# Quantising three weight matrices block by block inside a feed-forward loop, instead of each at once

## What is computed

```python
x = x + jnp.tanh(g_xattn[0]) * _L0_xattn_ref(...)   # a decaying recurrence (scan) over the tokens
x = x + jnp.tanh(g_ffn[0]) * _L0_ffn_ref(_layernorm(x), w1, w2, w3)
x = x + jnp.tanh(g_xattn[1]) * _L1_xattn_ref(_layernorm(x), ctx, wq, bq, wkv, bkv, wp, bp)
x = x + jnp.tanh(g_ffn[1]) * _L1_ffn_ref(_layernorm(x), gamma, W)

def _L0_ffn_ref(x, w1, w2, w3):              # _bitlinear: activations to 8 bits in groups of 64, weights to signs
    h = jax.nn.silu(_bitlinear(x, w1)) * _bitlinear(x, w2)
    return _bitlinear(h, w3)

def _qdq(x):                                  # in _L1_xattn_ref: of x, o (per token) and wq, wp (per output row)
    s = jnp.maximum(jnp.max(jnp.abs(x), axis=-1, keepdims=True) / 127.0, 1e-08)
    return jnp.clip(jnp.round(x / s), -127.0, 127.0) * s

# in _L1_ffn_ref: W to -1, 0, 1 by its mean magnitude
w_scale = 1.0 / (jnp.mean(jnp.abs(W)) + _EPS)
w_q = jnp.clip(jnp.round(W * w_scale), -1.0, 1.0) / w_scale
```

## Time and profile before

| | |
|---|---|
| median of 3 runs | 979.26 us (978.27 to 980.02) |
| profiled execution | 976.9 us |
| its span, first to last instruction | 975.0 us |
| mean granted TensorE clock | 0.948 of full speed |
| instructions | 15020 |
| PE, DVE, ACT, POOL busy | 822.8, 750.3, 576.2, 487.7 us |

### The profile page before, as it was taken

The page is one execution under the profiler, slowest core; times in us unless marked ns, Lnnn a source line. Parts: engine busy times, 40 slices in busy tenths (PEclk is TensorE's granted clock), DMA queues, the critical chain, the costliest instruction groups (busy, mean ns, idle before and its releaser), DMA issues.

```text
span 975.0 us, 15020 instructions
## 1 busy us (share of the span) xinstructions
PE 822.8 (84%) x4373; PEld 354.8 (36%) x4373; DVE 750.3 (77%) x1492; ACT 576.2 (59%) x971; POOL 487.7 (50%) x560
## 2 busy tenths in 40 slices
PE   2898997779698978999999978799999999974654
PEld 2444543334344434445444433132323232222321
DVE  4699998788598996888888767577777777624884
ACT  3588886544445654656566554466666666665762
POOL 2857662223244433434334344476767666664761
PEclk9999999899899998999999995999999999997885
DMA  8677875523424334232322342322222221000111
GB/s 285 207 197 209 218 196 155 151 69 66 108 55 109 59 54 84 54 65 54 64 55 54 66 75 76 88 56 61 70 63 68 61 72 46 1 1 1 43 65 65
DMA packets 172381, 86.37 MB, mean 89 GB/s; under 512 B 124048, under 2 KB 156960, under 8 KB 172320
## 3 DMA queue, kind: packets, MB, share of 16 engines
q1 hardware_dynamic: 172320, 85.64, 34.8%
HBM read 37.76 MB, written 12.58 MB: 52 GB/s over the span
## 4 chain that ended last, share of the span: by engine, by line
PE 43%; DVE 15%; issue 6%; SPq 6%; DMA 5%; ACT 4%; POOL 1%; ACTq 0%; DVEq 0%; POOLq 0%
PE bank L1109 13%; PE bank L1121 6%; PE bank L1203 5%; PE bank L1174 5%; PE bank L1193 4%; DMA A<-B 3%; PE bank L1320 2%; SPq L431 2%; PE bank L1222 2%; PE bank L1212 2%; DVE bank L1529 2%; SPq L455 2%; DVE gsm L1531 1%; DVE B L1534 1%; DVE B L1540 1%
## 5 line engine op out<-in xcount | busy, mean ns | idle before, releaser
L1109 PE MATMUL bank<-A,B 128*128 128x512 f16 x1024 | 236.0, 384 | 19.7 <-DVE B L1540 11.3
L1652 DVE TENSOR_REDUCE B<-bank 128x1 f32<-128x512 f32 x256 | 168.0, 683 | 71.7 <-PE bank L1174 71.6
L947 ACT ACTIVATE A<-bank 128x512 f32<-128x512 f32 x256 | 143.8, 593 | 105.5 <-PE bank L1193 102.5
L591 POOL TENSOR_TENSOR B<-B 128x512 f16<-128x512 f32 x64 | 76.0, 1188 | 225.2 <-ACT B L814 149.3
L1109 PEld LDWEIGHTS bank<-A,B 128*128 128x128 f16 x1024 | 100.7, 99 | 146.1 <-issue 21.8
L666 POOL TENSOR_TENSOR B<-A 128x512 f32<-128x512 f32 x64 | 79.3, 1270 | 93.8 <-ACT A L947 93.8
L1121 PE MATMUL bank<-A,B 128*128 128x512 f16 x512 | 121.9, 382 | 0.0
L809 ACT ACTIVATE bank<-B 128x512 f32<-128x512 f32 x64 | 38.5, 601 | 125.2 <-DVE B L1534 125.0
L1193 PE MATMUL bank<-A 98*128 98x512 f16 x256 | 93.8, 388 | 20.6 <-ACT A L947 10.9
L1174 PE MATMUL bank<-A 96*128 96x512 f16 x256 | 98.2, 409 | 7.8 <-DMA A<-B 4.2
L666 POOL TENSOR_TENSOR B<-B,A 128x512 f32<-128x512 f32 x64 | 79.1, 1266 | 0.5 <-ACT A L947 0.5
(11 more groups left out here) (216 smaller groups left out, 1465.0 us busy)
## 6 DMA issues: line engine op xcount, KB each, us to landing
B<-in_L_ffn_w_dram SPq DMA_DIRECT2D x48, 256.0 KB, 3.7
A<-k_parts SPq DMA_DIRECT2D x48, 128.0 KB, 2.5
A<-B SPq DMA_DIRECT2D x192, 32.0 KB, 1.9
X<-in_x_dram SPq DMA_DIRECT2D x4, 1024.0 KB, 9.1
B<-in_ctx_dram SPq DMA_DIRECT2D x16, 256.0 KB, 4.4
k_parts<-B SPq DMA_DIRECT2D x16, 256.0 KB, 4.4
v_rows<-B SPq DMA_DIRECT2D x16, 256.0 KB, 2.7
B<-v_rows SPq DMA_DIRECT2D x16, 256.0 KB, 3.2
```

The lines of the kernel that those rows point to most:

```text
L591: nc.gpsimd.tensor_tensor(HLb[j][:, 1, :], Db[j % 2], HLb[j][:, 0, :], ALU.subtract).then_inc(lo_done, 1)
L947: nc.scalar.activation(PR[(HG * t + j) % 8], bank[2 + j % 2][:, :], ACT.Exp, scale=SCALE).then_inc(exp_done, 1)
L1109: last = mm(bank[2 * n + q][:, :], XQT[a][:, m, :], wt[:, m % DB, j * 512:j * 512 + 512], start=(m == 0), stop=(m == 2 * DB - 1))
L1652: reduce(NMX[g % 2][:, t, j:j + 1], bank[ROW_BANKS[r % 3]][:, :], AX.X, ALU.max, negate=True).then_inc(row_max, 1)
```

## The change

The work on the three matrices is cut into twelve blocks (m, k), m the matrix, k one of its four quarters of 512 columns, and one block is done at the end of a chunk. `matrix_work(i, j, tiles_of)` names the block of a chunk: scales of matrix 0 in tile 1 and of matrix 2 in tile 7; roundings on ScalarE in tiles 2, 5 and 8; integers on VectorE and the transposes on SyncE in the same tiles, one chunk later (so the last one in tiles 3, 6, 9). `matrix_sum` moves to the end of chunk (3,3), `mean_scale` to the end of (4,3), the mean's product on TensorE to (4,2). The next matrix is loaded behind the last transpose of the one before, at (3,0) and (6,0). The scale row is written at (9,1) and read back at (11,1). TensorE's wait for `mean_scale` moves from `q_project(0)` to `q_project(1)`, and the mean's product gets a wait for `qf_ready`. Because the blocks stand in tiles up to 9, the loops over pairs 3 to 6 are written out on TensorE, VectorE, ScalarE and GpSimd.

```diff
-        ROUNDED, SUMMED = (1, 3, 4), 2
+        ROUNDED, SUMMED = lambda m, k: DB * m + k + (1 if m == 0 else 2), DB + 1
...
+        SCALED, ROUNDED_AT, INTS, SUMMED_AT = (1, 4, 7), (2, 5, 8), (2, 5, 8), 3
+
+        def matrix_work(i, j, tiles_of):
+
+            lag = 1 if tiles_of is INTS else 0
+            return [(m, k) for m in range(3) for k in range(DB) if DB * tiles_of[m] + k + lag == FC * i + j]
...
@@ SyncE @@
-            def turn_matrix(m):
-
-                sp.wait_ge(wm_ready, m + 1)
-                for k in range(DB):
-                    sp.dma_start_transpose((WQT, WLT, WPT)[m][:, :, k * P:k * P + P], wm_ints[:, k, :]).then_inc(wm_out, 16)
-            def spread_scale():
...
+            def turn_block(m, k):
+
+                sp.wait_ge(wm_ready, DB * m + k + 1)
+                sp.dma_start_transpose((WQT, WLT, WPT)[m][:, :, k * P:k * P + P], wm_ints[:, k, :]).then_inc(wm_out, 16)
             for i in range(TOK):
-                if i in (2, 4, 6):
-                    turn_matrix(i // 2 - 1)
-                if i in (2, 4):
-                    load_matrix(i // 2)
-                if i == 6:
-                    spread_scale()
                 for j in range(FC):
                     turn_h(i, j)
+                    for m, k in matrix_work(i, j, INTS):
+                        turn_block(m, k)
+                        if k == DB - 1 and m < 2:
+                            load_matrix(m + 1)
+                    if (i, j) == (INTS[2] + 1, 1):
+                        sp.dma_start(swp_dram.rearrange("(k p) -> p k", p=P), SWQP[:, 4:8],
+                                     allow_slow_non_contiguous=True).then_inc(swp_io, 16)
+                    if (i, j) == (INTS[2] + 3, 1):
+                        sp.wait_ge(swp_io, 16)
+                        sp.dma_start(swp_all[:, :], on_all(swp_dram, D)).then_inc(swp_io, 16)
                     if j == 0 and i < TOK - 1:
                         turn_x(i + 1, (i + 1) % 2)
...
@@ ScalarE @@
+            def round_block(m, k):
+
+                if k == 0:
+                    act.wait_ge(wm_scale, m + 1)
+                scale = WS if m == 1 else RWQP[:, (0, 0, 4)[m] + k:(0, 0, 4)[m] + k + 1]
+                nc.scalar.activation(wm_raw[:, k, :], wm_raw[:, k, :], ACT.Copy, bias=RND,
+                                     scale=scale).then_inc(wm_round, 1)
...
                         high(i, j)
+                        if (i, j) == (SUMMED_AT, FC - 1):
+                            matrix_sum()
+                        for m, b in matrix_work(i, j, ROUNDED_AT):
+                            round_block(m, b)
...
@@ TensorE @@
-                if isinstance(u, int) and u == 0:
+                if u == 0:
                     pe.wait_ge(wm_out, 16 * DB)
+                if u == 1:
                     pe.wait_ge(wm_scale, 2)
...
-                        if isinstance(k, int) and k == 1 and (a, j) == (0, 2):
+                        if (i, j) == (SUMMED_AT + 1, 2):
                             pe.wait_ge(wm_round, SUMMED)
+                            pe.wait_ge(qf_ready, 1)
                             mm(bank[7][:, 0:1], ones[:, :], PART[:, 3:4], start=True, stop=True).then_inc(setup_ps, 1)
...
@@ VectorE @@
+            def scale_block(m, k):
+
+                if k == 0:
+                    dve.wait_ge(wm_in, 16 * (m + 1))
+                c = (0, 0, 4)[m]
+                last_ = reduce(ABSM[:, c + k:c + k + 1], wm_raw[:, k, :], AX.X, ALU.max, apply_absolute_value=True)
+                if k == DB - 1:
+                    link(last_)
+                    link(ts(SWQP[:, c:c + 4], ABSM[:, c:c + 4], 1.0 / 127.0, 1e-8, ALU.mult, ALU.max))
+                    recip(RWQP[:, c:c + 4], SWQP[:, c:c + 4]).then_inc(wm_scale, 1)
...
+            def ints_block(m, k):
+
+                dve.wait_ge(wm_round, ROUNDED(m, k))
+                if k == 0:
+                    up_to(dve, wm_out, 16 * DB * m)
+                raw = wm_raw[:, k, :]
+                if m != 1:
+                    ts(wm_ints[:, k, :], raw, RND, 127.0, ALU.subtract, ALU.min).then_inc(wm_ready, 1)
+                else:
+                    link(ts(raw, raw, RND, -1.0, ALU.subtract, ALU.max))
+                    ts(wm_ints[:, k, :], raw, 1.0, None, ALU.min).then_inc(wm_ready, 1)
...
+                        for m, b in matrix_work(i, j, SCALED):
+                            if m != 1:
+                                scale_block(m, b)
+                            elif b == FC - 1:
+                                mean_scale()
+                        for m, b in matrix_work(i, j, INTS):
+                            ints_block(m, b)
...
-            tiles(0, False)
-            tiles(1, False)
-            tiles(2, False)
-            with pool.Fori(3, TOK // 2 - 1) as k:
-                step.turn(12, k - 3)
-                tiles(k, False)
-            step.turns_over(TOK // 2 - 4)
-            tiles(TOK // 2 - 1, True)
+            for k in range(TOK // 2):
+                tiles(k, k == TOK // 2 - 1)
```

More of the change, by code:

```diff
@@ L447, in load_matrix @@
                 else:
-                    sp.wait_ge(wm_ready, m)
+                    sp.wait_ge(wm_ready, DB * m)
                 sp.dma_start(wm_raw, tiled((wq, wl, wp)[m])).then_inc(wm_in, 16)
-            def turn_matrix(m):
-                sp.wait_ge(wm_ready, m + 1)
-                for k in range(DB):
-                    sp.dma_start_transpose((WQT, WLT, WPT)[m][:, :, k * P:k * P + P], wm_ints[:, k, :]).then_inc(wm_out, 16)
-            def spread_scale():
[L459 to L462, removed]
+            def turn_block(m, k):
+                sp.wait_ge(wm_ready, DB * m + k + 1)
+                sp.dma_start_transpose((WQT, WLT, WPT)[m][:, :, k * P:k * P + P], wm_ints[:, k, :]).then_inc(wm_out, 16)
             load_matrix(0)
@@ L868, in tiles @@
                         c = FC * i + j
[L869 to L872, removed]
                         if j == 0 and there(i - 3):
@@ L1159, in tiles @@
                             down(i - 1, j, 1 - a)
[L1161 to L1166, removed]
+            for k in range(TOK // 2):
+                tiles(k, k == 0, k == TOK // 2 - 1)
             def rows(b, g, n):
@@ L1588, in mean_scale @@
                 recip(WS, LSC).then_inc(wm_scale, 1)
-            def matrix_ints(m):
-                dve.wait_ge(wm_round, ROUNDED[m])
-                up_to(dve, wm_out, 16 * DB * m)
+            def ints_block(m, k):
[3 more added lines that the diff above has]
+                raw = wm_raw[:, k, :]
                 if m != 1:
-                    ts(wm_ints, wm_raw, RND, 127.0, ALU.subtract, ALU.min).then_inc(wm_ready, 1)
+                    ts(wm_ints[:, k, :], raw, RND, 127.0, ALU.subtract, ALU.min).then_inc(wm_ready, 1)
                 else:
-                    link(ts(wm_raw, wm_raw, RND, -1.0, ALU.subtract, ALU.max))
-                    ts(wm_ints, wm_raw, 1.0, None, ALU.min).then_inc(wm_ready, 1)
+                    link(ts(raw, raw, RND, -1.0, ALU.subtract, ALU.max))
+                    ts(wm_ints[:, k, :], raw, 1.0, None, ALU.min).then_inc(wm_ready, 1)
             def tiles(k, first, last):
@@ L1604, in tiles @@
                         c = FC * i + j
-                        if isinstance(k, int) and k < 3 and (a, j) == (0, 2):
-                            mean_scale() if k == 1 else matrix_scale(k)
-                        if isinstance(k, int) and k < 3 and (a, j) == (1, 1):
-                            matrix_ints(k)
                         hidden(c, j % 2)
@@ L1628, in tiles @@
                             q_max(i - 2)
-            tiles(0, True, False)
-            mix_over()
-            tiles(1, False, False)
-            tiles(2, False, False)
-            with dve.Fori(3, TOK // 2 - 1) as k:
-                step.turn(38, k - 3)
-                tiles(k, False, False)
-            step.turns_over(TOK // 2 - 4)
-            tiles(TOK // 2 - 1, False, True)
+                        for m, b in matrix_work(i, j, SCALED):
[5 more added lines that the diff above has]
+                            ints_block(m, b)
+            for k in range(TOK // 2):
+                if k == 1:
+                    mix_over()
+                tiles(k, k == 0, k == TOK // 2 - 1)
             residual(TOK - 2, 0)
```

6 lines of the change are left out of this document (removed).

## The result

The changed kernel takes 965.14 us in the median of 4 runs (962.86 to 966.97), the kernel before 979.64: a ratio of 0.985, with an interval of 0.9822 to 0.9879. That is 14.5 us less, forecast were 16.6 less and 962.7 us. The profiled execution took 966.35 with a span of 964.6; against the profiled one of before (976.9) that is 10.5 us. The difference between 10.5 and 14.5 lies in which executions were profiled: the one before was 2.7 us faster than its median, the one after 1.2 slower.

What follows compares the result with a forecast made beforehand. TensorE's floor bounds tiles 9 to 14; tiles 0 to 7 lose time in holes. Of 30.7 us to gain, VectorE's pace gives back 14.1, leaving 16.6: 962.7 us from a median of 979.26, range 954 to 968.

Steps and rivals of the forecast that it cites:

- the 14.1 of the sum: Time given back in tiles 1 to 9 as VectorE falls behind, 14.1 us off a possible gain of 30.7.
- the holes: TensorE's idle stretches and slow products in tiles 1 to 7, 28.6 us with small gaps; all three holes go.
- VectorE's pace: VectorE needs 21.5 us for a full feed-forward tile against TensorE's 22.11, so it has some 0.6 to spare.
- its steps: Losses against TensorE's floor: 7.5 us up to (5,1), 2.3 in tiles 5 and 6, 4.1 in tiles 7 to 9.
- the collisions: Integer blocks on VectorE and GpSimd's tensor_tensor shut each other out; blocks priced 13.1 us in all, lower bound 5.6.
- the tie at j=1: Integer block at j=1 comes about when GpSimd's L591 starts: waits 0 or 1.1 us, half taken.
- One sign: If the forecast is right, GpSimd's L591 takes over 2 us in some places.
- The new wait: q_project(1) waits for the mean's scale: some 3 us TensorE idle at tile 5; without it only 0.6 less.
- Loops written out: Straight code in tiles 6 to 13 on four engines, priced 0, bounds -0.2 to +0.2 us a tile.
- rival 1: Integer blocks fall between GpSimd's operations, 7.5 of the 13.1 us vanish: gain 24.1, time 955.2, chance 0.22.
- Rival 2: VectorE hides everything and TensorE runs at its floor throughout: gain 30.7 us, time 948.6, chance 0.06.
- Rivals 3 and 4: Every block waits in full, 973.8 us, chance 0.07; straight code in tiles 6 to 13 comes too slowly, 987, chance 0.03.

Runs made afterwards that it cites:

- loops_out: The kernel before with only the loops over pairs 3 to 6 written out on the four engines: 979.93 us, ratio 0.999.
- row_later: The kernel before with only the read-back of the scale row on SyncE moved from tile 6 to tile 8: 973.1 us, ratio 0.9925.
- row_ahead_x: The changed kernel with the write of the scale row ahead of (9,0)'s transposes instead of behind (9,1)'s: 963.77 us, ratio 0.9863.
- all_three: The changed kernel with all four edits: roundings one chunk ahead, integer blocks ahead of `scaled`, mean_scale at (4,2), prep_max ahead of `scaled`: 949.52 us, ratio 0.9687.

## Why the prediction was right, and where it was off

*The number and its parts.* The forecast was right to 2.4 us, partly by luck: two of its terms were off, in opposite directions. VectorE took back some 4 us more than the 14.1 of the sum, and the holes were worth more than the profile showed, by 2.4 us if the stretch of `loops_out` is taken, which lost 5 us more at tile 5 and 3 less at (3,3).

*The holes.* They go, as forecast, some 25 us with the slow products. Loading earlier took 9.4 us alone (0.0096 of 978.7), the place of the scale row 8.3 (0.0085). The cause of the third was read only in part: "the scale row was written at 351.98 and read back only at 360.80, and the hidden tile's and x tile's transposes stood behind". They stood behind SyncE's wait, and without it the x tile's landed 4.3 us earlier; the rest is the write itself, ahead of them in the DMA queue.

*VectorE's pace decides what is given back.* Shown: 8.4 to 8.9 us come back by the lag and the new place of the integer blocks, 5.2 to 5.7 by moving `prep_max`, nothing of TensorE's work changed. The forecast of 14.1 us given back was 18.5 by the stretch (30.7 less 12.2). By its steps: from the start of tile 1 to (5,1) 9.2 were lost against TensorE's floor, forecast 7.5; from there to tile 7 3.4, forecast 2.3; in tiles 7 to 9 5.6, forecast 4.1. VectorE's own pace shows which term was too small. In tiles 11 to 13, where VectorE has no matrix work, its first operation of a tile (L1516) comes every 21.51 us; 21.5 had been taken. But from (1,0) to (5,0) it took 91.3 us, forecast 90.2, in tiles 5 and 6 50.8, forecast 49.4, and in tiles 7 to 9 71.9, forecast 70.4: 4.0 more in all, in each of the three stretches with matrix work. The mechanism was right, the price of the matrix work on VectorE too low.

*What was missing from the sum.* The rounding in the same chunk: 2.6 us of waits, which cost 1.2 to 1.7 by the stretches and perhaps all of it. And an operation that I had left out of the collisions: the product of `bp_all` (L1508, at the start of tile 2) took 1.38 us where L1521 took 0.68 before, as the scale block ahead of it had pushed it into GpSimd's time.

```profile
L1508 DVE TENSOR_TENSOR bp_all<-bp_all,vec x1: 1384/1384/1384, 238.0 to 238.0; 128x512 f32<-128x512 f32 x1
```

That is the other half of the rule in the Trainium skill, GPSIMD Engine Reference, section Key points, which counts VectorE instructions with two SBUF inputs too; this one has two, and the trace agrees. By their own lines the integer blocks cost what was forecast, but not by the forecast parts: 13.1 were in the sum, the sixteen operations take 12.1 us by the trace, less some 1.3 of overlap, and only the 2.6 of waits make it 13.4. Of the 4.0 that is 0.3, and L1508 0.7; the other 3 us no run places. Within it the tie at j=1 was taken at half; it went to GpSimd, because of the rounding. One sign didn't come: L594 was to take over 2 us in some places, as L591 did, and its longest is 1.39; a block of 0.4 held it for 0.2.

*The new wait* came with 2.47 us, forecast 3, and its removal gave 0.5 to 1.0 by the stretches, forecast 0.6. *Loops written out* cost nothing. *Rivals*: rival 1 (blocks between GpSimd's operations) was not this kernel, but is near what the moved blocks make: 956.0, where it had 955.2, though they also fill some of VectorE's idle time and still meet L612 twice. Rival 2 is what all four edits make: 949.5, where TensorE's floor was put at 948.6. Rivals 3 and 4 fell.

## What to carry to other kernels

Work that is spread out still has to fit the engine that takes it: count that engine's own pace for a tile without the work first, as here its spare 0.6 us a tile decided how much of the removed holes was kept. Place a small VectorE operation by what GpSimd does at that moment, not only by its length; behind the same dependence it cost 0.4 or 0.9 to 1.1 us. A DMA of many single numbers goes behind the transfers that the next tile needs: not waiting for it helped here only in part, since what stood behind it in the queue still landed late. The same goes for a load of 1 MB.

## What the runs showed of the hardware

- A transpose issued 2 us behind a write of 512 single numbers to DRAM, on the same queue, landed 10.1 us after its issue, against a median of 3.2 (`row_later`); of two issued 3.8 and 6.5 us behind it, 4.7 and 4.2 (`row_ahead_x`).
- A transpose issued 0.7 us behind a load of 1 MB landed 6.2 to 8.0 us after its issue (changed kernel and `all_three`).
- VectorE's tensor_scalar on 512 columns and GpSimd's tensor_tensor hold each other up, and who starts first wins: a block that started behind L594 ended 0.28 us behind it (0.91 and 1.13 instead of 0.41), and with 248.04 against 248.08 it took 0.39 and L594 1.38 instead of 1.16.
- VectorE's tensor_tensor with two SBUF inputs took 1.38 instead of 0.68 in the same way; some forty reductions of 512 columns that overlapped such a GpSimd operation kept 0.65 to 0.69.
